# Attention's node sums with their operands exchanged, and a copy and a turn between sum and add

## The reference

```
s = jnp.einsum('edh,edh->eh', q[row], k[col])        # row = destination, col = source, 8 heads of 16
m = jax.ops.segment_max(s, row, num_segments=n)
p = jnp.exp(s - m[row])
z = jax.ops.segment_sum(p, row, num_segments=n)
attn = p / z[row]
out = jax.ops.segment_sum(attn[:, None, :] * v[col], row, num_segments=n)
```

## Time and profile before

| part | before |
|---|---|
| median of three runs | 2020.27 us |
| profiled execution / its span | 2023.76 / 2021.9 us |
| attention, first gather to end | about 1455 to 2020 us of the span |
| busy over the span: PE, PE weight load, DVE, ACT, POOL | 79%, 65%, 77%, 53%, 71% |
| the same, 1560 to 1960 us (share of 400 us) | 72%, 61%, 78%, 39%, 76% |
| chain that ended last, largest line | POOL G L2006, 14% of the span |

### The profile page before, as it was taken

The page is one execution under the profiler, slowest core; times in us unless marked ns, Lnnn a source line. Parts: engine busy times, 40 slices in busy tenths (PEclk is TensorE's granted clock), DMA queues, the critical chain, the costliest instruction groups (busy, mean ns, idle before and its releaser), DMA issues.

```text
span 2021.9 us, 36098 instructions
## 1 busy us (share of the span) xinstructions
PE 1604.1 (79%) x10160; PEld 1316.6 (65%) x10160; DVE 1556.4 (77%) x4756; ACT 1071.2 (53%) x2202; POOL 1439.1 (71%) x1482
## 2 busy tenths in 40 slices
PE   3978888888589998898399999897638767677777
PEld 2766676676477777777287877774427656566666
DVE  7877767676679998898377877777868877777776
ACT  3355546465487777775465655652554343434341
POOL 6777777777577777776777777772277777777772
PEclk9666666565689999999699999999955555555555
DMA  6232232323133433433434343432386555555551
GB/s 183 56 88 67 78 88 56 88 57 88 52 100 103 105 105 102 135 105 99 148 74 136 107 135 106 133 99 93 99 223 172 153 167 151 161 159 161 163 147 45
DMA packets 171435, 231.75 MB, mean 115 GB/s; under 512 B 48220, under 2 KB 123983, under 8 KB 170980
## 3 DMA queue, kind: packets, MB, share of 16 engines
q0 software_dynamic: 53376, 123.02, 22.0%
q1 hardware_dynamic: 116710, 104.76, 17.5%
q10 hardware_dynamic: 1154, 1.67, 0.3%
HBM read 196.52 MB, written 36.08 MB: 115 GB/s over the span
## 4 chain that ended last, share of the span: by engine, by line
POOL 20%; PE 15%; issue 8%; DVE 7%; DMA 3%; ACT 3%; SPq 1%; DVEq 0%; POOLq 0%; ACTq 0%
POOL G L2006 14%; POOL G L741 5%; PE p_d L860 4%; PE p_d L931 3%; PE p_g L918 3%; PE p_g L808 2%; DMA G<-kv_d,idx 2%; PE p_o L841 1%; DMA G<-h_d,idx 1%; DVE hs L2266 1%; PE p_w L2066 1%; DVE XH L2260 1%; SPq L687 1%; DVE PV L2319 1%; ACT agg L1202 1%
## 5 line engine op out<-in xcount | busy, mean ns | idle before, releaser
L741 POOL DMA_INDIRECT G<-h_d,idx x624 | 616.0, 987 | 215.8 <-issue 181.1
L2006 POOL DMA_INDIRECT G<-kv_d,idx x416 | 406.8, 978 | 162.2 <-issue 157.6
L741 POOL DMA_INDIRECT G<-in_x,idx x416 | 401.8, 966 | 131.7 <-issue 108.9
L808 PEld LDWEIGHTS p_g<-S,G 128*128 128x128 f32 x2080 | 352.5, 233 | 164.5 <-issue 97.5
L808 PE MATMUL p_g<-S,G 128*128 128x96 f32 (+1 forms) x2080 | 374.3, 314 | 101.6 <-DMA G<-in_x,idx 63.5
L1389 DVE SCALAR_TENSOR_TENSOR S<-con,rel,shared 128x96 f32<-128x96 f32 (+1 forms) x1040 | 261.5, 293 | 0.4
L1169 ACT ACTIVATE work<-con,lo_f 128x128 bf16<-128x128 f32 x416 | 143.2, 392 | 209.4 <-PE p_d L820 209.1
L1416 DVE TENSOR_TENSOR agg<-agg,p_g 128x96 f32 (+1 forms) x520 | 119.2, 229 | 162.0 <-PE p_g L808 149.3
L931 PE MATMUL p_d<-Sb,kv_s 128*128 128x288 f32 x728 | 218.9, 418 | 20.0 <-ACT kv_s L1161 11.8
L1507 DVE TENSOR_TENSOR work<-work,p_d 128x312 f32 (+1 forms) x416 | 180.4, 464 | 51.3 <-PE p_d L820 45.7
L2066 PE MATMUL p_w<-oh,PV 128*128 128x40 f32 x832 | 195.0, 410 | 24.8 <-DVE PV L2319 23.6
(11 more groups left out here) (324 smaller groups left out, 2934.5 us busy)
## 6 DMA issues: line engine op xcount, KB each, us to landing
dst_b<-in_dst_row SPq DMA_DIRECT2D x104, 240.0 KB, 3.1
work<-A_d SPq DMA_DIRECT2D x25, 800.0 KB
A_d<-work SPq DMA_DIRECT2D x12, 1600.0 KB, 7.7
G<-h_d,idx POOLq DMA_INDIRECT x624
G<-in_x,idx POOLq DMA_INDIRECT x416
kv_s<-low_d SPq DMA_DIRECT2D x52, 128.0 KB
G<-kv_d,idx POOLq DMA_INDIRECT x416, 2.8
kv_s<-low_d SPq DMA_DIRECT2D x52, 96.0 KB
```

What stands on the lines that cost most here:

```text
L741: pool.indirect_dma_start(G[:, n % GRING, :], None, l.table, bass.IndirectOffsetOnAxis(ap=l.places[:, c:c + 1], axis=0)).then_inc(s_arr[i ...
L808: last = pe.matmul(p_g[:, g % PB, 0:width], G[:, c % GRING, :], S[:, c % (SRING * GR), 0:width], start=(k == 0), stop=(k == GR - 1))
L2006: pool.indirect_dma_start(G[:, c % KRING, :], None, d["kv"], bass.IndirectOffsetOnAxis(ap=idx[:, c:c + 1], axis=0)).then_inc(s_arr[c // QC ...
```

## The change

The node sums of a quad are computed with the operands exchanged. Before, the weighted values (128 columns) were loaded as the stationary operand and the one-hots (40 columns) streamed; the result was [features, 40 nodes], in the form that agg has. Now the one-hots (40 columns) are loaded and the weighted values (128 columns) streamed, likewise for the 8 columns of weights; the result is [40 nodes, 136]. ACT copies it from PSUM to SBUF (`node_copy`), PE turns it with two transposes into the old place of p_w (`sums_back`), and DVE's `add` waits for that (s_back) instead of for the sums (s_mm). Every `add` stands one quad later in DVE's order: those of step k were quads 4k-8 to 4k-5, and are now 4k-9 to 4k-6. The waits in `window_sums`, `output_t`, `values`, `queries` and `rescale` are unchanged, and so are all gathers and loads.

```diff
@@ PE
             for c in range(QC):
-                pe.matmul(p_w[:, q % 2, 0:WA], PV[:, q % VRING, c, :], oh1[:, k % OH1, j * QC + c, :], start=(c == 0),
-                          stop=(c == QC - 1))
+                pe.matmul(p_w[0:WA, q % 2, X_NODE:X_NODE + D], oh1[:, k % OH1, j * QC + c, :], PV[:, q % VRING, c, :],
+                          start=(c == 0), stop=(c == QC - 1))
             for c in range(QC):
-                last = pe.matmul(p_w[0:HEADS, q % 2, WA:2 * WA], ps[:, k % 2, j * QC + c, :],
-                                 oh1[:, k % OH1, j * QC + c, :], start=(c == 0), stop=(c == QC - 1))
+                last = pe.matmul(p_w[0:WA, q % 2, X_NODE + D:X_NODE + D + HEADS], oh1[:, k % OH1, j * QC + c, :],
+                                 ps[:, k % 2, j * QC + c, :], start=(c == 0), stop=(c == QC - 1))
             last.then_inc(s_mm, 1)
+
+        def sums_back(q):
+            pe.wait_ge(s_rest, q + 1)
+            pe.transpose(p_w[:, q % 2, 0:WA], by_node[:, q % 2, 0:D], con[0:WA, C_ID:C_ID + WA])
+            pe.transpose(p_w[0:HEADS, q % 2, WA:2 * WA], by_node[:, q % 2, D:D + HEADS],
+                         con[0:WA, C_ID:C_ID + WA]).then_inc(s_back, 1)
...
                 if old:
+                    sums_back(4 * k - 8)
                     window_sums(4 * k - 7)
...
+                if old:
+                    sums_back(4 * k - 5)
                 if now:
                     queries(4 * k + 3)
@@ ACT
+        def node_copy(q):
+            act.wait_ge(s_mm, q + 1)
+            act.activation(by_node[:, q % 2, :], p_w[0:WA, q % 2, X_NODE:X_NODE + D + HEADS], ACT.Copy).then_inc(s_rest, 1)
...
                 if mid:
                     weights(k - 1)
+                if old:
+                    node_copy(4 * k - 5)
                 if nxt:
                     far(4 * k + 6)
                     hot(4 * k + 6)
@@ DVE
-            dve.wait_ge(s_mm, q + 1)
+            dve.wait_ge(s_back, q + 1)
...
                 if old:
                     values(4 * k - 6)
-                    if k > 2:
-                        rescale(k - 2)
-                    add(4 * k - 8)
+                if batch(k - 3):
+                    add(4 * k - 9)
+                if old and k > 2:
+                    rescale(k - 2)
```

More of the change, by code:

```diff
@@ L1904, in attention @@
     PV = sb("PV", [P, VRING, QC, D])
+    by_node = sb("by_node", [WA, 2, D + HEADS])
     zt = sb("zt", [P, 2, HEADS])
@@ L1920, in attention @@
     X_COL, X_DIF, X_OUT = 256, 258, 128
+    X_NODE = 2 * WA
     s_lay, s_keep = sem("s_lay2"), sem("s_keep")
@@ L1935, in attention @@
     s_end, s_go = sem("s_end2"), sem("s_go2")
+    s_rest, s_back = sem("a_rest"), sem("a_back")
+    more_sweep = range(s_back.num, s_rest.num + 1)
     def in_step(k):
@@ L2103, in body @@
                 if old:
+                    sums_back(4 * k - 7)
                     window_sums(4 * k - 6)
@@ L2109, in body @@
                 if old:
+                    sums_back(4 * k - 6)
                     window_sums(4 * k - 5)
@@ L2186, in body @@
             for k in STEPS:
-                mid, nxt = batch(k - 1), batch(k + 1)
+                mid, old, nxt = batch(k - 1), batch(k - 2), batch(k + 1)
                 if nxt:
@@ L2192, in body @@
                     act.activation(agg[:], agg[:], ACT.Copy, scale=cur[:, 2:3]).then_inc(s_keep, 1)
+                if old:
+                    node_copy(4 * k - 8)
                 if mid:
@@ L2195, in body @@
                     rows_copy(k - 1)
+                if old:
+                    node_copy(4 * k - 7)
+                if mid:
                     rows_ordered(k - 1)
+                if old:
+                    node_copy(4 * k - 6)
+                if mid:
                     columns_copy(k - 1)
@@ L2403, in vector @@
                 if old:
-                    add(4 * k - 7)
+                    add(4 * k - 8)
                     values(4 * k - 5)
@@ L2411, in vector @@
                 if old:
-                    add(4 * k - 6)
+                    add(4 * k - 7)
                 for t in in_step(k - 1):
@@ L2418, in vector @@
                 if old:
-                    add(4 * k - 5)
+                    add(4 * k - 6)
                 if mid:
@@ L2428, in vector @@
             dve.sem_clear(per_sweep)
+            dve.sem_clear(more_sweep)
             dve.sem_inc(s_sweep, 1)
```

## The result

The changed kernel takes 2126.84 us (2119.73 to 2128.25, four runs) against 2021.45 for the one before: a ratio of 1.0499, 95% interval 1.0481 to 1.0518. The forecast was 2123. The profiled execution is the shortest of the four, 2119.73 with a span of 2118.0, 96.1 longer than the span before; the medians are 105.4 apart. So some 9 us of the difference stand in no trace kept here.

The account below looks back on a forecast made before the run. POOL's gather beat, 20.5 us per step, bounds the kernel; the later adds make a 24.8 us ring. Steps 77, other steps 11 and end 15 add 103 to the profiled 2023.76: 2127, or 2123 as a median; range 2100 to 2148, chance 0.78.

Parts of the forecast that it names:

- POOL's beat: Attention before the change: one gather per 1.283 us, sixteen per step, sets the step at 20.5 us.
- the ring: Closed chain of waits through one attention step, from add(4k-5) to the next such add: 24.8 us instead of 20.5.
- segments 1, 2, 3 and 5: Add(4k-5) to products 4.0 us; products to add(4k-4) 6.4; that add to segment_max 3.8; add(4k-3) to values(4k-4) 4.7.
- rival B: PE's clock rises in attention: at 2.4 GHz 19.2 us, total 2023, chance 0.04; in part 2040 to 2100, chance 0.08.
- upper bound: Matmul load and stream add up, 3.3 us per quad's sums: 27.1 us per step, total 2176.
- segment 1: Add(4k-5) to products, with output tile's turn, sums of 4k-4 and turn of scores and queries on PE: 4.0 us.
- segment 5: Add(4k-3) to values(4k-4), with sums of 4k-1, then ACT's node_copy, far, hot and the weights' copy: 4.7 us.
- full steps: 18 of 22 attention steps pay the whole 4.3 us lengthening, 77 us.
- the others: First step 3.0 us, step without output tile 0.6, the one after 4.1, last with products 3.4: 11 together.
- the end: From the last batch's first product to the last normalise: 57.5 us against 42.75, so 15 more.
- The lengthening is covered (A): Attention steps stay at 20.5 us and only the end pays: total 2035, chance 0.05.
- C: PE's clock at the upper level through to the end, so the kernel gets faster: total 2014, chance 0.05.

Follow-up runs that it names:

- both edits: Changed kernel with the output tile's turn behind the next window sums on PE and ACT's node_copy behind the weights' copy: 2054.78 us, 1.0145 times the kernel before.

## Why the prediction was right

1. *POOL's beat sets the step before, and DVE has 3 to 4 us of it free.* Shown: with fewer gathers the step is 16.34, against 16.3 counted as DVE's own work along the ring.
2. *The exchanged matmuls cost what the old ones did, 2.54.* Nearly: from the first sums at 1791.22 to the next work at 1793.56 they take 2.34. The price of a pass is as forecast: successive large passes start 0.213 apart (median) in both traces, with 128 columns loaded and 40 streamed as with 40 loaded and 128 streamed. What is saved lies at the edges. Before, with the first load at 1770.01:

```profile
1770.11 1.87 PE L2066 MATMUL p_w<-oh,PV 128*128 128x40 f32 x8
...
1771.92 0.70 PE L2069 MATMUL p_w<-oh,ps 128*8 128x40 f32 x8
```

From that load to the first small pass are 1.91 us; in the changed kernel load and stream start together, and it is 1.72. This is the term that was mis-sized, by 0.2. The ring holds four of these sums, in segments 1, 2, 3 and 5, and not three as the forecast's bounds and its rival B count; with 3.3 for each, its upper bound is 27.8 and not 27.1. In segment 1 the 0.2 does not show, because the tile's two turns take 0.61 there (1790.61 to 1791.22) where the forecast had 0.48. The added work is near the forecast: ACT's copy takes 0.28 for 0.26, the two turns of a quad's sums 0.39 (1794.39 to 1794.78) for 0.45.

3. *The order costs, in six segments, 24.8.* Measured 23.99, each segment within 0.3. That it is the order is shown by running it alone; that 2.4 of segment 1 are the sums behind the output tile's wait, and 0.7 of segment 5 the place of ACT's copy, is shown by moving each. The waits of the window sums for their bank (segments 3 and 5) stand in the list of waits, 87.7 us, but were not taken out by themselves.
4. *Where it pays.* The forecast had 77 from full steps, 11 from the others and 15 from the end. From the first product of the first batch to that of the last the changed kernel takes 572.0, the one before 491.3: 80.7. Most steps repeat after 23.9 to 24.1, 3.5 over 20.4, and 18 of these make 63. What is left of the 80.7, 18, is more than forecast: the kernel before catches up in its third and fourth step (17.74 and 15.16 after a late start), and the changed kernel does not (21.02 and 22.71). The end is 56.64 after the last batch's first product, against 42.75: 13.9, forecast 15. The two errors, steps too dear and edges too cheap, cancel in part. That is luck, and so is some of the closeness of 2123 to 2126.84: the forecast added 103, where the two profiled executions lie 96.1 apart and the medians 105.4. The first products are the first two rows here, of the kernel before and the changed one; the last two rows are the end of the changed one.

```profile
1484.32 0.69 DVE L2260 TENSOR_TENSOR XH<-p_qe,G 128x512 f32<-128x512 f32 x1 [2.09 <-PE p_qe L2031]
...
1485.48 0.69 DVE L2289 TENSOR_TENSOR XH<-p_qe,G 128x512 f32<-128x512 f32 x1 [2.07 <-PE p_qe L2035]
...
2057.51 0.69 DVE L2289 TENSOR_TENSOR XH<-p_qe,G 128x512 f32<-128x512 f32 x1 [3.51 <-PE p_qe L2035]
...
2113.81 0.34 DVE L2399 TENSOR_SCALAR XH<-XH,mv,rstd 128x128 f32<-128x128 f32 x1 [0.35 <-ACT rstd L2201]
```

5. *The rivals.* The lengthening is covered (A) only where the adds stand in their old places: there the step is 20.40, and in the changed kernel it is 23.9. The clock (B, C) stayed at 0.51 from 1560 to 1960.

## What to carry to other kernels

Before an instruction that publishes a result is moved later, list who waits for it and what stands behind each waiter in its own engine's stream: here the adds moved by a quad, their waiters did not, and 2.3 us of matmuls that needed nothing stood behind one of them. Free time on the engines of a loop that waits for transfers can cover new work (here two turns on PE and a copy of 0.28 us on ACT for each quad, for 0.3% in all), but not a ring of waits through three engines; add up one turn of it by rows and compare that with the loop's period. Here the loop left the beat that had set its step, and the busy shares of all engines went down at once.

## What the runs showed that was not expected

The granted clock, 0.50 throughout this part before, rose to 1.0 for short times in some of the kernels that stream 128 columns: four times in the changed kernel's attention, 0.51 on the mean, and twelve times with both edits, 0.54 from 1560 to 1860. Two stretches of the changed kernel (columns as in the earlier trace rows), and its PE in both: a quad's large passes, from their start to that of the small ones, took 0.96 us in the first and 1.70 in the second.

```profile
1776.00:1778.00 2.00, 0.36 (x4) 0.39 (x5) 1.97 (x10) 0.66 (x2) 1.70 (x2) 1.00 0.35 109
1782.00:1784.00 2.00, 1.77 (x10) 1.62 (x10) 1.97 (x5) 0.33 (x2) 1.47 (x2) 0.50 0.48 142
```

```profile
1777.64 1.17 PE L2070 MATMUL p_w<-PV,oh 128*40 128x128 f32 x8 [1.86 <-DVE agg L2376]
1778.60 0.69 PE L2073 MATMUL p_w<-ps,oh 128*40 128x8 f32 x8
...
1782.23 1.90 PE L2070 MATMUL p_w<-PV,oh 128*40 128x128 f32 x8 [1.78 <-DVE agg L2376]
1783.93 0.69 PE L2073 MATMUL p_w<-ps,oh 128*40 128x8 f32 x8
```

A full step of the changed kernel with such a moment in it takes 23.2 to 23.4 instead of 23.9 to 24.1. There are three of these, so in this execution it is worth some 2 us. What raises the clock is not shown. With the order alone, 40 columns streamed, it stayed at 0.50; but so it did in the changed kernel with fewer gathers, which streams 128.
